# A convolution on VectorE in half-unit skew, with ScalarE seeding all but two units, in a routed expert kernel

## The reference

```python
def _L0_cond_ref(x, w, b):
    y = jax.lax.conv_general_dilated(x, w, window_strides=(1,), padding=[(K - 1, 0)], feature_group_count=D, ...)
    return y + b

def _L0_ffn_ref(x, w_router, w_experts):
    logits = jnp.einsum('bsh,eh->bse', x, w_router)
    idx = jnp.argmax(logits, axis=-1)
    all_out = jnp.einsum('bsh,efh->bsef', x, w_experts)
    return jnp.take_along_axis(all_out, idx[:, :, None, None], axis=2)[:, :, 0, :]

x = x + _L0_ffn_ref(_L0_cond_ref(x, cond_2048[:, None, :], L0_cond_b), L0_ffn_w_router, L0_ffn_w_experts)
```

## Time and profile before

| | us |
|---|---|
| median of three runs | 599.31 |
| the runs | 595.94 to 601.25 |
| the profiled execution, its own time | 599.66 |
| its span, first to last instruction | 598.0 |
| busy in the span: TensorE, VectorE, ScalarE, GpSimd | 546.1, 348.2, 192.9, 221.2 |

### The profile page before, as it was taken

How to read it: one execution, slowest core, us unless ns; L and a number is a source line. 1 busy time by engine, 2 the same in 40 slices (tenths; PEclk the granted TensorE clock), 3 DMA queues, 4 the chain that set the end, 5 groups by cost and what they waited for, 6 DMA issues and landing times.

```text
span 598.0 us, 10202 instructions
## 1 busy us (share of the span) xinstructions
PE 546.1 (91%) x3151; PEld 456.9 (76%) x3152; DVE 348.2 (58%) x404; ACT 192.9 (32%) x361; POOL 221.2 (37%) x222
## 2 busy tenths in 40 slices
PE   9999997789799987999899999999999999999930
PEld 7988886669688765788778888888888888888830
DVE  7999999449079561243887433275348332755720
ACT  7764654425390000012545110051015100514200
POOL 1300898765637722332222233321432242324321
PEclk9999999869999989799989999999999999999975
DMA  8734738626888359454998956368558754795451
GB/s 349 277 111 151 266 122 272 237 73 251 285 258 329 95 175 360 169 159 157 329 379 273 317 176 198 118 224 303 176 172 289 242 175 141 221 305 176 130 186 36
DMA packets 54936, 129.44 MB, mean 216 GB/s; under 512 B 7936, under 2 KB 29056, under 8 KB 54656
## 3 DMA queue, kind: packets, MB, share of 16 engines
q0 software_dynamic: 17616, 55.10, 26.3%
q1 hardware_dynamic: 15840, 54.42, 25.9%
q10 hardware_dynamic: 21456, 19.60, 12.0%
HBM read 93.45 MB, written 40.52 MB: 224 GB/s over the span
## 4 chain that ended last, share of the span: by engine, by line
PE 53%; DMA 4%; issue 2%; DVE 1%; ACT 1%; ACTq 1%; POOL 0%; POOLq 0%; DVEq 0%
PE ps L1099 53%; DMA out<-x_row,ids_first 2%; DMA x_row<-x_rows,idx 2%; ACT w_sb L522 1%; DMA out<-x_row,idx 1%; DVE w_sb L842 0%; ACTq L364 0%; POOL x_row L1183 0%; DVE x_row L870 0%; DVE ys L862 0%; DVE y_cols L857 0%; POOLq L1208 0%; DVEq L879 0%; DMA idx_in_sb<-id_sorted 0%; POOL idx L1214 0%
## 5 line engine op out<-in xcount | busy, mean ns | idle before, releaser
L1099 PE MATMUL ps<-w_sb,ys 128*128 128x512 f32 x1680 | 388.9, 394 | 11.2 <-DVE ys L862 6.3
L1099 PEld LDWEIGHTS ps<-w_sb,ys 128*128 128x128 f32 x1680 | 318.9, 190 | 80.1 <-issue 10.3
L857 DVE STREAM_TRANSPOSE y_cols<-y_blk 128x1024 f32<-128x1024 f32 x37 | 46.0, 1244 | 165.1 <-PE ps L1099 141.1
L541 ACT CAST ys<-y_cols 128x1024 fp32r<-128x1024 f32 x37 | 39.1, 1057 | 284.1 <-DVE y_cols L857 258.9
L684 DVE SCALAR_TENSOR_TENSOR y_pre<-x_all,cst,y_pre 128x1024 f32<-128x1024 f32 x72 | 87.3, 1288 | 0.1
L975 PE MATMUL ps<-x_all,bands 128*128 128x128 f32 x640 | 78.2, 279 | 4.0 <-issue 3.9
L975 PEld LDWEIGHTS ps<-x_all,bands 128*128 128x128 f32 x640 | 74.0, 193 | 7.5 <-issue 7.4
L842 DVE TENSOR_TENSOR w_sb<-w_raw,w_sb 128x1024 fp32r<-128x1024 f32 x56 | 64.2, 1220 | 20.2 <-ACT w_sb L522 17.3
L1190 POOL DMA_INDIRECT out<-x_row,idx x32 | 37.6, 1175 | 86.4 <-DVE x_row L870 80.9
L1214 POOL COPY idx<-idx_in_sb 128x1 int32<-128x1 int32 x34 | 9.3, 273 | 147.5 <-DMA out<-x_row,idx 136.4
L522 ACT CAST w_sb<-w_raw 128x1024 fp32r<-128x1024 f32 x56 | 53.9, 1048 | 21.5 <-PE ps L1099 15.5
(11 more groups left out here) (130 smaller groups left out, 208.7 us busy)
## 6 DMA issues: line engine op xcount, KB each, us to landing
w_raw<-experts SPq DMA_DIRECT2D x56, 512.0 KB
y_blk<-y_sorted ACTq DMA_DIRECT2D x148, 128.0 KB
x_all<-x_t SPq DMA_DIRECT2D x32, 520.0 KB, 6.0
w_lead<-experts SPq DMA_DIRECT2D x8, 512.0 KB
bands<-conv_full SPq DMA_DIRECT2D x2, 1024.0 KB, 10.9
y_blk<-y_sorted SPq DMA_DIRECT2D x8, 128.0 KB
idx_in_sb<-id_sorted POOLq DMA_DIRECT2D x36, 1.0 KB
x_row<-x_rows,idx POOLq DMA_INDIRECT x34
```

The source lines that it names most:

```text
L541: nc.scalar.copy(ys[:, HI, k, :, :].rearrange("p c s -> p (c s)"), y_cols[k][:, :, :].rearrange("p c s -> p (c s)")).then_inc(ys_hi, 1)
L857: V.transpose(y_cols[k][:, :, :].rearrange("p m (t i) -> p t m i", t=4), y_blk[:, k, :, :, :]).then_inc(y_blocks, 1)
L1099: mm = nc.tensor.matmul(out_ps[k][:, f * HALF:(f + 1) * HALF], ys[:, a, k, c, :], w_sb[:, (b * HC + c) * H + f * HALF:(b * HC + c) * H + ( ...
```

## The change

The order of the taps on VectorE no longer takes the units in pairs; each unit starts when the one before it is half done. ScalarE seeds units 2 to 11, where it seeded 2, 4, 6, 8 and 10. The seeds stand at three places of each group on ScalarE: before the copies of the turned chunks 0 and 1 (g > 0) or after `copy_conv(0, 4)`, before `copy_rows(g, 3)`, and before `copy_rows(g, 7)`. `choose` and `place_rows` stand at other numbers of taps. The x of each VectorE unit is loaded by itself, and not two together.

```diff
 def seeded_by_act(m):
-    return m > 0 and m % 2 == 0
+    return m >= 2
 def tap_order():
-    order, done, marks = [], {}, 0
-    for pair in range(0, DVE_UNITS, 2):
-        last = {m: done.get(m - PRE_RING) for m in (pair, pair + 1)}
-        for k in (FIRST_TAP, *range(FIRST_TAP)):
-            for m in (pair, pair + 1):
-                if k == FIRST_TAP and seeded_by_act(m):
-                    continue
-                order.append((m, k, last[m]))
...
+    when = []
+    for m in range(DVE_UNITS):
+        if not seeded_by_act(m):
+            when.append((FIRST_TAP * m - 2, m, FIRST_TAP))
+        when += [(FIRST_TAP * m + 2 * k, m, k) for k in range(FIRST_TAP)]
+    order, last, end, marks = [], {}, {}, 0
+    for _, m, k in sorted(when):
+        order.append((m, k, last.get(m)))
+        marks += GROUP if k == LAST_TAP else 1
+        last[m] = marks
+        end[m] = len(order)
+    return order, last, end
+ROUTE_AFTER = (10, 13, 15)
@@ SyncE
-                if n in (6, 8, 11, 14):
-                    load_dve(m)
-                    load_dve(m + 1)
-                    m += 2
+                if n in (4, 5, 7, 8, 10, 11, 13, 14):
+                    load_dve(m)
+                    m += 1
...
-            sp.wait_ge(taps_done, TAPS_DONE[DVE_UNITS - 2])
-            load_lead(e, LEAD_ORDER[0])
-            sp.wait_ge(taps_done, TAPS_DONE[DVE_UNITS - 1])
-            for c in LEAD_ORDER[1:4]:
+            for n, c in enumerate(LEAD_ORDER[0:4]):
+                sp.wait_ge(taps_done, TAPS_DONE[min(DVE_UNITS - 3 + n, DVE_UNITS - 1)])
                 load_lead(e, c)
@@ ScalarE, for g in range(LAST)
                     copy_conv(g, 4)
+                    seed(dve_unit(g + 1, N_PE))
                 else:
                     copy_conv(g, 3)
                     copy_conv(g, 4)
+                    seed(dve_unit(g + 1, N_PE))
                     copy_rows(g, 0)
-                    seed(4 * g + 2)
                     copy_rows(g, 1)
                 copy_rows(g, 2)
                 copy_rows(g, 5)
+                seed(dve_unit(g + 1, N_PE + 1))
                 copy_rows(g, 3)
-                if g + 1 < LAST:
-                    seed(4 * g + 4)
                 if g + 1 < LAST:
                     copy_conv(g + 1, 0)
                 copy_rows(g, 4)
                 copy_rows(g, 6)
                 if g + 1 < LAST:
                     copy_conv(g + 1, 1)
+                seed(dve_unit(g + 1, N_PE + 2))
                 copy_rows(g, 7)
                 copy_parts(g)
@@ VectorE
-            add_taps(PAIR + NEXT)
-            add_taps(6)
-            choose(0)
...
+            for g in range(LAST):
+                n = UNIT_END[dve_unit(g, HC - 1)] + ROUTE_AFTER[g]
+                add_taps(n)
+                choose(g)
+                add_taps(n + 2)
+                place_rows(g)
             find_lead()
-            add_taps(NEXT - 8)
+            add_taps(len(TAP_ORDER))
```

More of the change, by code:

```diff
@@ L67, in seeded_by_act @@
 def seeded_by_act(m):
-    return m > 0 and m % 2 == 0
+    return m >= 2
 def tap_order():
-    order, done, marks = [], {}, 0
-    for pair in range(0, DVE_UNITS, 2):
-        last = {m: done.get(m - PRE_RING) for m in (pair, pair + 1)}
-        for k in (FIRST_TAP, *range(FIRST_TAP)):
-            for m in (pair, pair + 1):
-                if k == FIRST_TAP and seeded_by_act(m):
-                    continue
-                order.append((m, k, last[m]))
[L83 to L86, removed]
+    when = []
[10 more added lines that the diff above has]
+    return order, last, end
 FIRST_TAP, LAST_TAP = TAPS - 1, TAPS - 2
-TAP_ORDER, TAPS_DONE = tap_order()
-PAIR = 2 * TAPS
-NEXT = PAIR - 1
+TAP_ORDER, TAPS_DONE, UNIT_END = tap_order()
+ROUTE_AFTER = (10, 13, 15)
 LAST = GROUPS - 1
@@ L665, in _, with add_taps @@
             at = [0]
-            def add_taps(n):
-                for m, k, last in TAP_ORDER[at[0]:at[0] + n]:
+            def add_taps(end):
+                for m, k, last in TAP_ORDER[at[0]:end]:
                     c = m % N_DVE
@@ L675, in add_taps @@
                     if k == 0 and seeded_by_act(m):
-                        dve.wait_ge(seeded, m // 2)
+                        dve.wait_ge(seeded, m - 1)
                     if k == FIRST_TAP:
@@ L695, in add_taps @@
                                                op0=ALU.mult, op1=ALU.add).then_inc(taps_done, 1)
-                at[0] += n
+                at[0] = end
             steps = [0]
```

## The result

The kernel after took 612.45 us (median of four runs, 610.93 to 613.98) beside 598.63 (595.94 to 601.25) for the kernel before: a ratio of 1.0231, interval 1.0178 to 1.0284. Its profiled execution took 610.93 us with a span of 609.3, 11.3 more than the 598.0 of before.

What follows compares the result with a forecast made beforehand. It took the route from `choose(2)` through scatter and row loads to TensorE's first product as bounding; +2.0 there and -1.0 for weights gave +1.0 us: 600.7 profiled, 600.3 on the median, stated as 600.5 us, range 594.5 to 607.

Steps and rivals of the forecast that it cites:

- The waits for seeds: VectorE waits before tap 0 of units 6, 8 and 9 for ScalarE's seeds: 2, 5.1 and 4 us or more.
- `copy_parts` behind a seed: A seed ahead of `copy_rows(g, 7)` delays `copy_parts` by 1.2 us; TensorE idles 0.9 more, for g = 0 and 1.
- `choose(2)`: VectorE ready at 132.3 to 136.0, TensorE's logits at 136.7; the later counts: taken as 135.9, 2.0 us later.
- The sum: +2.0 us at `choose(2)` and -1.0 for the first weights' loads: +1.0 us on the profiled execution.
- the event whose shift reaches the end one to one: `place_rows(2)` and `choose(2)` before it, through scatter and row loads to TensorE's first product at 173.56.
- 8.78 us of slack: VectorE's wait for TensorE's logits before `choose(2)` in the kernel before; the forecast had it used up.
- The weights: First weights' loads go out 6 to 7 us earlier, sharing DMA with group 2's scatter: -1 us, bounds -2 and +2.
- GpSimd freed: Faster rival: without `tensor_scalar` after unit 1, scatters go up to 18 us earlier; 596.0 us; 20% together with early seeds.
- VectorE carries the lateness: Slower rival: VectorE has no slack left, so late releases reach `choose(2)`, 5.8 us later; 605.5 us, 25%.
- its point: The slower rival, with late releases on VectorE, decides once seed 9 comes after 106.4 us.
- Seeds early enough: Rival: ScalarE's copies run ahead, `choose(1)` at 89 to 91, end at 597 to 598 us; 20% together with freed GpSimd.
- a case that starts at 593.5: The faster case, freed GpSimd or early seeds, from 593.5 to 598 us, 20%.

Runs made afterwards that it cites:

- experiment 3: Kernel after with the seeds of units 6, 8 and 9 moved earlier on ScalarE: 592.45 us, ratio 1.0007 to the kernel before.
- experiment 1: Both kernels again without edit, on another chip, without slow stretches: after 602.0 us against 593.15 for before, ratio 1.0168.
- Experiment 6: First four lead weight loads held until conv 19 or 20 of 20: after 600.36 (600.01 on another chip) or 606.67 us; before, held to 20, 592.49.
- experiment 7: Kernel before with first taps of units 3, 5, 7, 9, 11 as `scalar_tensor_tensor` instead of `tensor_scalar`: 595.48 us beside 597.33, no ratio.
- experiment 5: Kernel after, unedited, in five rounds on a chip with slow stretches: 611.3 us against 598.47 for before, ratio 1.0227.
- 4's second run: Kernel after with the three seeds earlier and `choose(2)` seven entries earlier, repeated on another chip with more runs: 587.54 us, ratio 0.9823 to before.
- 8: Kernel before with the x of VectorE's units loaded one by one: 599.99 us, ratio 1.0151, not resolved.
- 9: Kernel after with the eight id scatters of group 2 held until TensorE's last convolution: 605.8 us, ratio 1.0215 to before.

## Why the prediction was wrong

**The waits for seeds: right in place and nearly in size.** Forecast 2 (1.7 to 2.5), 5.1 (4.1 to 6.1) and 4 or more, measured 2.96, 5.47 and 5.40. `choose(1)` was forecast at 95.1 and came at 96.30. `copy_parts` behind a seed cost TensorE 0.70 us; I had 0.9. Moving the seeds forward gave 9.6 us back (experiment 3).

**`choose(2)`: right for VectorE, wrong for TensorE.** VectorE was forecast at 132.3 to 136.0 and arrived at 134.41. But I put TensorE's logits at 136.7, "if its slow stretch stays as it is"; they were done at 124.9, because the stretch was not there any more. I took the later of two numbers that I thought close; they were 9.5 us apart. That the sum came near (135.9 against 134.41) is partly luck.

**The sum: here it failed.** It had one route from `choose(2)` to the end: "the event whose shift reaches the end one to one", with "TensorE's product is tied to it by this route even if its own convolutions finish early". The route itself came out as summed: +0.5 at `choose(2)`, +0.2 at the second block (I had +1.0). What I left out is the other side, that TensorE's own queue may finish late. The trace of before spoke against that step already: TensorE had no idle time before its first product, and the rows were ready 0.46 us earlier. A longer wait of TensorE was forecast at `rank(1)` only (2.07 us against 1.40); `rank(2)`, where it waited 7.44 us instead of not at all, is not in the prediction, and so had no price. From `rank(2)` to the first product TensorE took 46.8 us (135.92 to 182.73) instead of 36.3 (137.30 to 173.56), 10.5 more. Its slow `conv` took 15.0 us where that of before took 8.5, the work at the lower clock after the wait some 2 us more, and the rest are slower instructions and short waits behind them. Less the 1.4 us by which `rank(2)` came earlier, that is the +9.2, and it is not in my sum.

**The base of the sum was one execution's.** The 8.78 us of slack on VectorE belonged to a slow stretch that comes and goes. Without it (experiment 1) the slack is 1.80, the limit is GpSimd, and of VectorE's loss of 15.9 us 5.4 are left at the scatter and 6.1 at the first product. The change is slower on either kind of chip (1.0231 and 1.0227; 1.0168 and 1.0155), and on either I would have needed another base.

**The weights: wrong sign, small.** I took -1, bounds -2 and +2. Between scatter and the loads of rows it is 22.8 us in after and 21.2 in before (first executions): +1.6. Experiment 6 shows why: those bytes push the rows back some 5 us when they lie beside the scatter. In before they did so as well, so the change adds only the difference. The row behind this term also showed it: the loads of 149.09 went out while the scatter from 139.51 was still running, and did not follow it.

**The rivals.** *GpSimd freed* was right in its mechanism: the hold went (experiment 7), and the next groups' scatters went out on time. It was wrong as a gain, since the scatter of group 2 waits for VectorE's positions. *VectorE carries the lateness* was right in sign, and seed 9 came after its point (107.17 against 106.4), but `choose(2)` wasn't late by it: in the first execution its mechanism isn't what happened. Without slow stretches VectorE does carry the loss (`choose(2)` 15.9 us later), by the waits for seeds and the place of `choose(2)` and not by late releases without a name. *Seeds early enough* didn't occur. No case of mine had TensorE's queue in it, so the range ended at 607. The hold of 19.56 us lasted across sixteen other VectorE instructions, twelve of 128x1024 and four of 128x512, not twelve. And the chances contradict each other: 11% for faster than 593.3 doesn't fit under a case that starts at 593.5 with only 5% beyond both ends.

**Open.** What the slow stretches are. They stood in all six traces from the chips of the first executions, of experiments 5 and 4's second run, and of 7 and 8, and in none of the eleven traces from the three other chips. Each chip was used at one time only, so chip and time can't be told apart. A low clock is not what starts them: in after it stands at 1.00 until 154 us, with 20 matmuls issued from 148 on, and near 0.50 only after that, and experiment 5 shows much the same. The profile has queues that load instructions; between 148 and 164 us they moved one packet in after and two in the execution of experiment 1 without a stretch, so nothing there tells the two apart. Experiments 6 and 9 were meant to test the weights and the ids as the cause, and fell on chips without a stretch. No run here shows what starts them. So it is shown that the places of the seeds and of `choose(2)` make the change slower than before, on either kind of chip, and it is open why the stretch in after is longer than those of before.

## What to carry to other kernels

A helper engine's output that another engine waits for must be placed by when it is wanted, not where the helper's loop has room: three seeds behind copies cost over 9 us, and moving them alone returned it. Before using a slack from a trace, look at whether the engine that sets it was running normally (matmuls per stretch, granted clock), and read a second execution: here 8.78 us of slack were 1.80. When a wait grows on the engine that bounds the kernel, sum its own queue to the end as well as the route by which the data comes.

## What the runs showed of the hardware

- TensorE can go through stretches in which it issues 25 to 40 matmuls in 16 us (40, 36 and 25 in three executions), where undisturbed executions issued 156 to 165, with no wait on record. The granted clock averaged 0.68 to 0.71 over these 16 us, but was still 1.00 in the first 4 to 6 of them. With them the first product of one kernel came 7 to 9 us later; on three other chips there were none.
- After 8.3 us without work TensorE's granted clock was 0.50 for the next 3.3 us (136.7 to 140), and 0.70 over the 16 us from 132 to 148 in which the wait ended, against 1.00 where it had not waited.
- A GpSimd DMA instruction beside VectorE's `tensor_scalar`s of 128x1024 was on record for 19.56 us, over sixteen other VectorE instructions (18.55 and 16.66 us in two variants of before). With `scalar_tensor_tensor` in their place the same one took 1.86, and its neighbours up to 2.10 instead of 0.97.
- Four loads of 512 KB from SyncE's queue beside GpSimd's scatter of a group put off the loads of the scattered rows by 5 us (21.5 against 16.2; 21.1 against 16.4).
